# Inverse DFT columns with the table as the weight and one image at a time, in a vision tower on one core

## The reference, cut to what matters

```
for sw, cw, cb in ((sw0, cw0, cb0), (sw1, cw1, cb1), (sw2, cw2, cb2), (sw3, cw3, cb3)):
    x1 = _spectral_conv(x, sw)      # rfft2, 20x20 modes times sw, irfft2
    x2 = jnp.einsum('bchw,oc->bohw', x, cw) + cb[None, :, None, None]
    x = _gelu(x1 + x2)
```

## Time and profile before

| | us |
|---|---|
| median of 3 runs | 1164.38 (1162.56 to 1165.36) |
| profiled execution, its own time | 1165.57 |
| its span in the trace | 1163.8 |
| TensorE matmuls busy | 1067.9 (92%) |
| VectorE busy | 623.3 (54%) |
| ScalarE busy | 409.6 (35%) |
| GpSimd busy | 124.5 (11%) |

### The profile page before, as it was taken

One profiled execution on the slowest core, in us unless ns is written; L12 is line 12 of the kernel. 1 busy time (PEld: TensorE's weight loads), 2 busy tenths in 40 slices (PEclk: granted clock), 3 DMA queues, 4 the chain that ended last, 5 costly groups with the idle time before them and its releaser, 6 DMA issues.

```text
span 1163.8 us, 34246 instructions
## 1 busy us (share of the span) xinstructions
PE 1067.9 (92%) x15860; PEld 710.2 (61%) x15860; DVE 623.3 (54%) x782; ACT 409.6 (35%) x554; POOL 124.5 (11%) x112
## 2 busy tenths in 40 slices
PE   5899999999999999999899999999999899678896
PEld 4577767767776633677677767767325788522221
DVE  2248445823844322458338545833144577789787
ACT  2332233133223386231232223123586777321100
POOL 6000000000000000000000000020000755211511
PEclk9999999999999999999999999999899999789999
DMA  5220130022012400310220031020011000000000
GB/s 182 87 73 3 36 110 17 2 87 73 3 39 64 131 6 24 111 30 3 87 73 2 13 119 31 3 87 16 2 24 41 2 2 1 1 1 1 5 5 10
DMA packets 25652, 46.62 MB, mean 40 GB/s; under 512 B 9437, under 2 KB 10488, under 8 KB 24869
## 3 DMA queue, kind: packets, MB, share of 16 engines
q1 hardware_dynamic: 24694, 43.49, 12.4%
q10 hardware_dynamic: 384, 0.66, 0.2%
q0 software_dynamic: 432, 0.29, 0.1%
HBM read 30.25 MB, written 10.89 MB: 35 GB/s over the span
## 4 chain that ended last, share of the span: by engine, by line
PE 74%; DVE 13%; ACT 3%; issue 3%; DMA 3%; POOL 2%; SPq 1%; ACTq 0%; POOLq 0%; DVEq 0%
PE PSALL L1221 22%; PE PSALL L1080 9%; PE PSALL L1189 7%; PE PSALL L1097 7%; DVE WORK L1413 5%; PE PSALL L1299 4%; PE PSALL L1212 4%; PE PSALL L1165 4%; PE PSALL L1309 3%; PE PSALL L494 2%; PE PSALL L397 2%; DVE WORK L949 2%; DMA WORK<-MIXED 2%; DVE WORK L1432 2%; PE PSALL L482 2%
## 5 line engine op out<-in xcount | busy, mean ns | idle before, releaser
L1432 DVE STREAM_TRANSPOSE WORK<-PSALL 128x1024 f32<-128x1024 f32 x128 | 152.4, 1229 | 319.6 <-PE PSALL L1189 319.6
L1221 PEld LDWEIGHTS PSALL<-EW,WORK 64*128 64x128 f32 x4096 | 250.5, 193 | 65.5 <-issue 48.4
L1221 PE MATMUL PSALL<-EW,WORK 64*128 64x128 f32 x4096 | 266.7, 283 | 12.8 <-DVE WORK L1432 12.8
L1349 ACT ACTIVATE X<-PSALL,TABLES 128x1024 f32<-128x1024 f32 x128 | 141.7, 1114 | 333.6 <-PE PSALL L1221 333.6
L1413 DVE STREAM_TRANSPOSE WORK<-PSALL 128x1024 f32<-128x1024 f32 x100 | 119.1, 1230 | 58.4 <-PE PSALL L1080 54.6
L1097 PE MATMUL PSALL<-TABLES,WORK 128*128 128x128 f32 x1000 | 138.4, 287 | 4.9 <-DVE WORK L1413 0.5
L1097 PEld LDWEIGHTS PSALL<-TABLES,WORK 128*128 128x128 f32 x1000 | 120.7, 194 | 32.1 <-issue 18.4
L1330 ACT COPY SPEC<-PSALL 128x400 f32<-128x400 f32 x64 | 53.5, 846 | 175.5 <-PE PSALL L1097 172.3
L1080 PE MATMUL PSALL<-WORK,DW 32*64 32x256 f32 x3200 | 103.3, 389 | 12.6 <-DMA B<-in_fc_b 12.6
L1409 DVE STREAM_TRANSPOSE WORK<-X 128x1024 f32<-128x1024 f32 x96 | 111.4, 1204 | 0.0
L949 DVE TENSOR_TENSOR WORK<-PSALL,X 128x832 f32<-128x832 f32 x80 | 80.4, 1019 | 16.6 <-PE PSALL L482 15.7
(11 more groups left out here) (146 smaller groups left out, 962.1 us busy)
## 6 DMA issues: line engine op xcount, KB each, us to landing
SW<-in_spec_w SPq DMA_DIRECT2D x160, 80.0 KB, 2.8
spec_scr<-MIXED SPq DMA_DIRECT2D x24, 400.0 KB, 3.3
SPEC<-spec_scr SPq DMA_DIRECT2D x32, 200.0 KB
WORK<-spec_scr SPq DMA_DIRECT2D x16, 200.0 KB
WORK<-MIXED SPq DMA_DIRECT2D x64, 40.0 KB
WORK<-in_coords_w SPq DMA_DIRECT2D x2, 1024.0 KB, 4.9
XC<-in_coords_c SPq DMA_DIRECT2D x2, 1024.0 KB, 7.2
hid_scr<-WORK SPq DMA_DIRECT2D x64, 8.0 KB
```

What stands on the lines that cost most here:

```text
L1221: m = pe.matmul(PS[2 * p + z][:, 2 * b * GRID:(2 * b + 2) * GRID], G[64 * z:64 * z + 64, n % 2, b, h:h + 4, :, c].rearrange("p q o -> p (q ...
L1349: nc.scalar.activation(X[:, n].rearrange("p b (z d) c w -> p d z b (c w)", z=2)[:, p, :, :, 2 * t * GRID:2 * (t + 1) * GRID], PSALL[:, 2 * ...
L1432: nc.vector.transpose(G[:, n % 2, 2 * x + y].rearrange("p h o v -> p o h v"), PSALL[:, 4 + 2 * x:6 + 2 * x, :].rearrange("p k (h o v) -> p ...
```

## The change

The inverse half of a layer is turned round. The table EW becomes the weight (64 rows x 32 columns) and the image's data G moves, 256 columns at a time; eight tiles of 64x32 are possible, four on each half of the array's rows. Each half (z) of an image writes one bank (6 or 7); VectorE transposes that bank into bank 2*(i%2)+z, PSUM to PSUM, 128x512 (`inverse_columns_out`); and the pixel weights are then added onto it (`image_pointwise`, start=False), with weights of 64 rows of which one half is zero (`TABLES[..., 0]` for the one and `ODD` for the other; `W0` gets a second, masked copy). Inverse rows are made for one image at a time, in banks 4 and 5 and on the row half that holds its modes (x = i % 2). `arm()` runs four dense matmuls in banks 0 to 3 in place of `keep_busy`, so that later matmuls add. Everything goes image by image: ih_full, g_ready, x_full and x_ready count 16 per layer, and ic_full and t_ready are new. For odd images the columns of the next image's first half are issued before the wait for the second transpose. `columns(0)` and `first_columns_dft` now follow behind the last image; of the next layer's pixel transposes two are put behind images 13 and 14 on VectorE. The scratch tiles smx, emx and rden of the tail move into E0.

The diff, cut to its core:

```diff
-            def inverse_rows(l, n, y):
-                if n == 0 and y == 0:
+            def place(i):
+                y, x = i // 2 % 2, i % 2
+                return i // B4, y, x, 2 * x + y
+            def arm():
+                for bank in range(4):
+                    pe.matmul(PS[bank], ident[:], work[:, 0:BANK], start=True, stop=True)
+            def inverse_rows(l, i):
+                n, y, x, b = place(i)
+                if i == 0:
                     turn.wait(mix_ready, N_MIX)
                     turn.wait(straight_in, 1)
-                elif y == 0:
+                elif i % B4 == 0:
                     turn.wait(loaded[n], 1)
-                if n or y:
-                    turn.wait(g_ready, 4 * n + 2 * y)
-                for a, b in ((0, 8), (8, MODES // 2)):
+                if i:
+                    turn.wait(g_ready, i)
+                for a, b, bank, at in ((0, 8, 4, 0), (8, MODES // 2, 5, 0)):
                     for z in range(2):
-                        for x in range(2):
-                            m = pe.matmul(PSALL[64 * z:64 * z + 64, 4 + 2 * x + a // 8, 0:(b - a) * 2 * CH],
-                                          TABLES[64 * x:64 * x + 64, l, EH0 + 64 * z:EH0 + 64 * z + 64],
-                                          MODE[n % 2][64 * x:64 * x + 64, y, a:b, :],
-                                          start=True, stop=True, tile_position=(64 * x, 64 * z))
+                        m = pe.matmul(PSALL[64 * z:64 * z + 64, bank, at:at + (b - a) * 2 * CH],
+                                      TABLES[64 * x:64 * x + 64, l, EH0 + 64 * z:EH0 + 64 * z + 64],
+                                      MODE[n % 2][64 * x:64 * x + 64, y, a:b, :],
+                                      start=True, stop=True, tile_position=(64 * x, 64 * z))
                 m.then_inc(ih_full.sem, 1)
...
+            def image_columns(i, z):
+                n, y, x, b = place(i)
+                for w in range(2):
+                    for q in range(4):
+                        m = pe.matmul(PS[6 + z][Q * q:Q * q + Q, 256 * w:256 * w + 256],
+                                      EW[64 * z:64 * z + 64, GRID + Q * w:GRID + Q * w + Q],
+                                      G[64 * z:64 * z + 64, n % 2, b].rearrange("p (m q) o v -> p q m v o", q=4)[:, q],
+                                      start=True, stop=True, skip_group_check=True, tile_position=(64 * z, Q * q))
+                        if w and q == 3:
+                            m.then_inc(ic_full.sem, 1)
+                        yield
+            def image_pointwise(l, i, z):
+                n, y, x, b = place(i)
+                row, image = slice(64 * z, 64 * z + 64), n * B4 + b
                 for p in range(2):
-            def keep_busy(count):
+                    for q in range(4):
+                        m = pe.matmul(PS[2 * (i % 2) + z][Q * q:Q * q + Q, 256 * p:256 * p + 256],
+                                      TABLES[row, l, ODD if p else 0:(ODD if p else 0) + CH] if l else W0[row, p, 4 * (image // OCT) + q, :],
+                                      X[row, n, b, q].rearrange("p c w -> p (c w)") if l else
+                                      XC[row, image % OCT].rearrange("p c w -> p (c w)"),
+                                      start=False, stop=True, skip_group_check=True, tile_position=(64 * z, Q * q))
+                        if z and q == 3 and p:
+                            m.then_inc(x_full.sem, 1)
+                        yield
+            def issue(*parts):
+                for _ in itertools.zip_longest(*parts):
+                    pass
             def layer(p, l):
                 if l:
                     forward(l)
                     cols.next()
                 mix()
-                pointwise(l, 0, 0)
-                keep_busy(3)
-                inverse_rows(l, 0, 0)
-                for n in range(NG):
-                    for t in range(SETS):
-                        if n == NG - 1 and t and l < LAYERS - 1:
-                            columns(0)
-                        if n == NG - 1 and t and l == LAYERS - 1 and p + 1 < PASSES:
-                            first_columns_dft()
-                        if n or t:
-                            pointwise(l, n, t)
-                        if n or t:
-                            inverse_columns(n, t)
-                        else:
-                            first_columns(l)
-                        if n + 1 < NG:
-                            inverse_rows(l, n + 1, t)
+                arm()
+                inverse_rows(l, 0)
+                inverse_rows(l, 1)
+                issue(image_columns(0, 0), image_columns(0, 1))
+                if l == 0:
+                    passes.wait(xc_in, 1)
+                for i in range(GIMG):
+                    if i + 2 < GIMG:
+                        inverse_rows(l, i + 2)
+                    elif i + 1 < GIMG:
+                        turn.wait(g_ready, GIMG)
+                    turn.wait(t_ready, 2 * i + 1)
+                    if i + 1 == GIMG:
+                        issue(image_pointwise(l, i, 0))
+                        turn.wait(t_ready, 2 * i + 2)
+                        issue(image_pointwise(l, i, 1))
+                    elif i % 2:
+                        issue(image_columns(i + 1, 0))
+                        turn.wait(t_ready, 2 * i + 2)
+                        issue(image_columns(i + 1, 1), image_pointwise(l, i, 0))
+                        issue(image_pointwise(l, i, 1))
+                    else:
+                        turn.wait(t_ready, 2 * i + 2)
+                        issue(image_columns(i + 1, 0), image_columns(i + 1, 1))
+                        issue(image_pointwise(l, i, 0), image_pointwise(l, i, 1))
+                if l < LAYERS - 1:
+                    columns(0)
+                elif p + 1 < PASSES:
+                    first_columns_dft()
...
-            def activated(l, n, t, p):
-                turn.wait(x_full, 4 * n + 2 * t + p + 1)
+            def activated(l, i):
+                turn.wait(x_full, i + 1)
                 nc.scalar.activation(
-                    X[:, n].rearrange("p b (z d) c w -> p d z b (c w)", z=2)[:, p, :, :, 2 * t * GRID:2 * (t + 1) * GRID],
-                    PSALL[:, 2 * p:2 * p + 2, :].rearrange("p z (b n) -> p z b n", b=B4),
+                    X[:, i // B4, 2 * (i % 2) + i // 2 % 2].rearrange("p q c w -> p (q c w)"),
+                    PSALL[:, 2 * (i % 2):2 * (i % 2) + 2, :].rearrange("p z n -> p (z n)"),
                     ACT.Gelu, bias=TABLES[:, l, BIAS:BIAS + 1]).then_inc(x_ready.sem, 1)
...
             def pixels_onto_partitions(k):
                 n, b = k // B4, k % B4
-                if k == 0:
-                    turn.wait(x_full, 12 - 4 * NG)
-                turn.wait(x_ready, 4 * (n + 1) - 4 * NG)
+                if k < 2:
+
+                    turn.wait(x_ready, B4)
+                else:
+                    turn.wait(x_ready, 4 * (n + 1) - 4 * NG)
                 if k >= 4:
                     cols.wait(c_full, (k - 4) // 2 + 1)
...
             def first_weights():
                 firsts.wait(w0_full, 1)
-                nc.vector.tensor_copy(W0[:].rearrange("p a b -> p (a b)"), PS[3][:, 0:OCT * CH]).then_inc(w0_ready.sem, 1)
+                for odd in range(2):
+                    m = nc.vector.tensor_scalar(W0[:, odd].rearrange("p a b -> p (a b)"), PS[3][:, 0:OCT * CH],
+                                                TABLES[:, 0, MARK + odd:MARK + odd + 1], None, ALU.mult)
+                m.then_inc(w0_ready.sem, 1)
                 firsts.next()
-            def inverse_rows_out(n, y, x):
-                if x == 0:
-                    turn.wait(ih_full, 2 * n + y + 1)
-                    if n >= 2 and y == 0:
-                        turn.wait(x_full, 4 * (n - 1))
-                nc.vector.transpose(G[:, n % 2, 2 * x + y].rearrange("p h o v -> p o h v"),
-                                    PSALL[:, 4 + 2 * x:6 + 2 * x, :].rearrange("p k (h o v) -> p (k h) o v", o=CH, v=2)
+            def inverse_rows_out(i):
+                turn.wait(ih_full, i + 1)
+                nc.vector.transpose(G[:, i // B4 % 2, 2 * (i % 2) + i // 2 % 2].rearrange("p h o v -> p o h v"),
+                                    PSALL[:, 4:6, :].rearrange("p k (h o v) -> p (k h) o v", o=CH, v=2)
                                     .rearrange("p h o v -> p o h v")
                                     ).then_inc(g_ready.sem, 1)
+            def inverse_columns_out(i, z):
+
+                turn.wait(ic_full, 2 * i + z + 1)
+                if i >= 2:
+                    turn.wait(x_ready, i - 1)
+                nc.vector.transpose(PSALL[:, 2 * (i % 2) + z, :].rearrange("p (m h w) -> p h m w", h=2, w=Q),
+                                    PSALL[:, 6 + z, :].rearrange("p (h m o) -> p h m o", h=2, o=CH)
+                                    ).then_inc(t_ready.sem, 1)
+
             def layer(l):
                 if l:
```

(14 more changed lines are left out.)

90 lines of the change are left out of this document (22 added, 68 removed).

## The result

The changed kernel takes 1270.81 us (median of 4 runs, 1266.61 to 1272.11) where the kernel before, run beside it, takes 1164.87: ratio 1.0902, 95% interval 1.0866 to 1.0937, so 9% slower. The profiled execution took 1272.11 us around a span of 1270.3. Predicted were 1256 and a range of 1215 to 1292.

A forecast was written before the change was run, and what follows sets the result against it. TensorE was taken to bound the inverse half and VectorE the forward half. 1165.6 + 66 (layer ends) + 9.2 and 6.7 (pass ends) + 9.6 (clock) = 1257, given as 1256 against the median of runs; range 1215 to 1292.

The forecast's parts named there:

- The step on which all hung: Inverse half: a new tile shape empties the whole array first, so inverse rows, 1.22 us per image, overlap with nothing.
- The first rival: Inverse half: array halves overlap across shapes, 5.2 to 5.7 us per pair, about 1151 us in all; chance 0.15.
- The pair: Inverse loop, two images: even turn 3.21 us plus odd turn 4.11, 7.3 where the old step takes 6.37.
- The transposes and ScalarE: Inverse half: new PSUM-to-PSUM transposes take 0.7 us each and VectorE stays hidden; ScalarE, 1.1 per image, hidden too.
- The third rival: Inverse half: VectorE does not hide if a transpose exceeds 1.23 us; 0.4 per pair per 0.1 us; within the remaining 0.04.
- The start: Start of a layer's inverse half: arm() costs nothing; single PSUM delays rows of image 2 by 5.40 us; no clock fall charged.
- The end: End of a layer: 12.15 us from image 14's turn to second-round transposes, 11.0 later than before; 66 over six layers.
- the end of pass 0: Image 14's turn to the first dense matmul takes 8.15 us; that matmul comes 9.2 later than before.
- the end of pass 1: Image 14's turn to the first dense matmul takes 4.8 us; that matmul comes 6.7 later than before.
- The clock: Layer ends: TensorE idles 2.5 us, one fall to the lower clock each, 6 x 1.6 = 9.6 us; none at starts.
- a rival with 13 more: Clock falls at all eight layer starts, 13 us more, and longer at ends, 10 more; up to 1290; chance 0.11.

The follow-up runs named there:

- e2_rows_32: Changed kernel with inverse rows on 64x32 tiles, the shape of columns and pointwise, with twice the instructions of half the width: 1200.44 us, ratio 1.0260.
- e5_rows_32_even: Changed kernel with inverse rows on 64x32 tiles and the even images' order for every image: 1195.91 us, ratio 1.0275.
- e8: Changed kernel with one more VectorE transpose of 128x416 per image, its result not used: 1275.07 us, ratio 1.0948.
- e3: Changed kernel with useless dense matmuls in three idle stretches of TensorE per layer, behind arm(), image 0's rows and columns(0): 1226.21 us, ratio 1.0507.

## Why the prediction was right

**The step on which all hung holds.** "A new shape empties the whole array first" is what the loop shows (the 0.41 and 0.17 us of issue, 1.22 us per image in which nothing of another shape starts), and e2_rows_32 and e5_rows_32_even show it from the other side: shape alone changed, and a pair fell from 6.98 to 5.7 in the odd order, a turn from 3.15 to 2.85 in the even one. The first rival named 5.2 to 5.7 per pair for halves that overlap. With one shape the loop comes to the upper end of that, but e5 comes there almost without overlap, so the rival's 5.45 was not reached and its arithmetic not confirmed. By TensorEngine Tiling (Array Packing) of the Trainium skill, Key Properties, changing the tiling mode drains TensorE: these runs agree, and they show that 64x64 to 64x32, the same row halves and only narrower, counts as such a change.

**The pair was over-sized.** Predicted 3.21 + 4.11 = 7.32, measured 3.17 + 3.81 = 6.98. The even turn was right. In the odd turn I counted twelve records in sequence behind the rows; within one shape the free half goes ahead (the 26 loads at 295.81), so columns on half 1 do not wait for all of those on half 0. That is my reading of the 0.30 us that came off. Seven pairs: 2.4 us a layer less, 19 in all.

**The transposes and ScalarE** were right: 0.70 us taken, 702 ns measured; VectorE hidden in the loop (e8). The third rival falls.

**The start** was right but for the clock: 5.40 us were predicted until the rows of image 2, 281.11 - 274.74 = 6.37 measured, and 5.3 in e3 (266.35 - 261.06), with the clock held up.

**The end** was right with the same reserve: 12.15 predicted, 13.25 measured (346.97 - 333.72), and 1.56 less in e3; idle time of TensorE 2.5 predicted, 2.55 measured. At the end of pass 0 it was 457.93 - 449.64 = 8.29 from image 14's turn to the first dense matmul against 8.15, at the end of pass 1 933.15 - 928.21 = 4.94 against 4.8.

**The clock was under-sized, and that is the term that failed.** I charged 6 falls of 1.6 us at the ends, 9.6, and put the eight starts at nothing; a fall at every start was left to a rival with 13 more. The ends were priced well: 10.7 by e3_fill_idle. The low clock came at all eight starts too and lasted longer than the one that I had read the earlier trace rows, 10.24 us at six of them: 31.2 us, more than twice that rival's price. With 3.6 in the fully connected stage it is 45.5 in place of 9.6, and 44.6 by the medians of e3_fill_idle.

**The sum again with what was measured.** Time from inverse half to inverse half (first matmul of the inverse rows), in us of the profiled executions:

| | before | after | more | predicted |
|---|---|---|---|---|
| the first three layers of each pass, together | 612.6 | 693.8 | 81.2 | 66 + 9.6 |
| last layer of pass 0, to pass 1's first | 117.7 | 132.8 | 15.0 | 9.2 |
| last layer of pass 1, to the end | 390.7 | 400.9 | 10.2 | 6.7 |

That makes 106 us more (the first inverse half starts at the same time) against the 91.5 predicted. By e3_fill_idle, whose clock is as high as that of the kernel before, the change without the clock costs 1226.21 - 1166.12 = 60 us where 82 were predicted, and the clock 45 where 9.6 were. So the near agreement of 1256 and 1271 rests on two errors of opposite sign, 22 too much (19 of them in the pairs) and 35 too little. The direction and the mechanism of the loop were foreseen; that the size came out so near is luck.

**What stays open.** Why the clock fell at these starts. Rows on half the array do not do it alone (the loop stays at 1.00), and filling the waits cures it. But the waits alone do not do it either: the kernel before has the same two in every layer. These are the two of its second layer, with the window from there on (granted clock 1.00):

```profile
144.92 1.31 PE L1189 MATMUL PSALL<-WORK,TABLES 64*64 64x512 f32 x16 [0.73 <-DMA WORK<-MIXED]
...
147.59 1.21 PE L1221 MATMUL PSALL<-EW,WORK 64*128 64x128 f32 x16 [1.36 <-DVE WORK L1432]
...
144.90:155.10 10.20, 8.59 (x120) 5.88 (x128) 4.80 (x5) 1.77 (x2) 0.00 (x0) 1.00 0.52 170
```

Its first waits are 0.24 to 1.64 us and its second 1.36 to 1.44, and seven of its eight starts kept the clock; the changed kernel has 0.48 to 1.80 and 1.34 to 1.42, and none did. A start with 0.73 and 1.36 before kept it, one with 0.48 and 1.34 after lost it. So neither the number nor the length of the waits tells the kernels apart. What differs is the work between and behind them: inverse rows of two images on both halves of the array before, of one image on one half after. Whether that decides, no run shows: none changed it alone.

## What to carry to other kernels

Before giving a step its own tile shape, count the changes of shape per turn and cost the step as time in which the array does nothing else; an equal shape with twice the instructions was worth 59 us here with the clock held up, and an order written for overlap across shapes costs time where there is none to be had. Where an engine is the bound and the change opens short waits at a stage's ends, ask for the granted clock of that stage and fill the waits with dense matmuls before judging the change: here that was worth 45 us of 1271. Ask it of the stage's start as well as of its end: the ends were priced here and the starts were not. When a move of data to another engine takes away cover at the end of a stage (here the first forward rounds), the next stage's first step can be put back in front of the last step of this one.

## What the runs showed of the hardware

- The drain at a change of tile shape counts in the width too: 64x64 to 64x32 on the same rows left 0.17 us of issue ahead of the first load, and the way back 0.41; with one shape neither is there, and a turn in the same order takes 2.85 us in place of 3.15.
- Within one shape a half of the array runs ahead of the other: with 64x32 tiles throughout, loads of inverse rows and of columns alternate (269.91 to 270.61 in e2_rows_32).
- A transpose of 128x512 float32 from PSUM to PSUM takes 702 ns on VectorE, 128x416 from PSUM to SBUF 582.
- Two waits of 0.51 and 1.34 us, 1.3 us of work on half the array between them, were followed by 10.24 us at 1.2 GHz although TensorE was busy for all of these. Two waits of 0.73 and 1.36 us with work on both halves between them, in the kernel before, were followed by no fall. TensorE: Matmul & The Clock Gate of the Trainium skill, in A second HAM failure mode, describes short idle times between groups of matmuls that make the clock swing. The starts of the changed kernel's layers agree with it, and its loop, which has no idle time, stays at 2.4 GHz; seven of the eight starts of the kernel before, with idle times as short, show no fall.
